# Expanding K and V for two heads at a time, and an output stage without its GpSimd copy, in an eight-core attention and LoRA-mixture layer

## What is computed

```
q    = rms(x @ wq_a.T) @ wq_b.T              # 32 heads of 64 + 64
ckv  = x @ wkv_a.T                           # 256 latent + 64 rotary key
kv   = rms(ckv[..., :256]) @ wkv_b.T         # 32 heads of 64 (k_nope) + 128 (v)
k    = concat(k_nope, rope(ckv[..., 256:]))  # the rotary part is shared by all heads
attn = softmax(causal(q @ k.T * scale)) @ v
x1   = ln(x + attn @ wo.T)
gate = softmax over the top 16 of 64 expert scores of x1
z    = (x1 @ A.T) * gate repeated over the 8 ranks of an expert
out  = ln(x1 + 2 * (z @ B.T))
```

## Time and profile before

| | us |
|---|---|
| median of 2 runs | 4685.25 (4610.16 and 4760.34) |
| the profiled execution | 4619.39 |
| its span, slowest core (core 6) | 4617.9 |
| spans of the other cores | 4577.5 to 4606.9 |
| stage D | about 1156 to 3394 |
| output stage | about 4494 to 4618 |

### The profile page before, as it was taken

One profiled execution on the slowest core, in us unless ns is written; L12 is line 12 of the kernel. 1 busy time (PEld: TensorE's weight loads), 2 busy tenths in 40 slices (PEclk: granted clock), 3 DMA queues, 4 the chain that ended last, 5 costly groups with the idle time before them and its releaser, 6 DMA issues.

```text
span 4617.9 us, 53437 instructions; the slowest of 8 cores (4577.5 to 4617.9 us)
## 1 busy us (share of the span) xinstructions
PE 2834.0 (61%) x19214; PEld 1381.3 (30%) x19214; DVE 1019.6 (22%) x1923; ACT 1232.6 (27%) x1280; POOL 402.4 (9%) x482
## 2 busy tenths in 40 slices
PE   2772744443666676666666666666678888718650
PEld 0220211111333343333333343333333333203110
DVE  0110000000232322222222323323310000161126
ACT  0000001111445444444444444444420000000110
POOL 4431002233000000000000000000010000000004
PEclk9886877777899989999999999999999999858765
DMA  8777240001100000000000000000053333110003
GB/s 123 110 99 108 38 71 2 0 0 27 19 1 1 1 1 1 1 1 1 1 1 1 1 1 1 1 1 1 1 82 83 86 82 85 41 38 0 0 5 141
DMA packets 76492, 145.66 MB, mean 32 GB/s; under 512 B 12306, under 2 KB 53396, under 8 KB 70228
## 3 DMA queue, kind: packets, MB, share of 16 engines
q0 software_dynamic: 65488, 107.90, 15.0%
q1 hardware_dynamic: 10756, 34.34, 1.9%
HBM read 233.31 MB, written 16.78 MB: 54 GB/s over the span
## 4 chain that ended last, share of the span: by engine, by line
PEldq 32%; issue 17%; PEld 15%; DVE 15%; ACT 7%; DMA 3%; another core or an unknown queue 3%; DVEq 2%; POOLq 2%; POOL 2%; ACTq 1%; SPq 0%
PEldq L267 32%; DVE AR L267 15%; ACT AR L267 7%; PEld mix L267 4%; PEld psE L267 3%; PEld sA L267 3%; DVEq L267 2%; POOLq L267 2%; POOL AR L267 2%; PEld psL L267 1%; ACTq L267 1%; DMA AR<-wqbT 1%; DMA AR<-xoT 1%; DMA out<-AR 1%
## 5 line engine op out<-in xcount | busy, mean ns | idle before, releaser
L267 PE MATMUL sA<-AR 128*128 128x128 bf16 (+2 forms) x3200 | 520.9, 285 | 194.1 <-DVEq L267 57.8
L267 PE MATMUL mix<-AR 128*128 128x129 bf16 x5120 | 411.8, 224 | 259.9 <-DVEq L267 172.5
L267 PE MATMUL psE<-AR 128*128 128x512 bf16 x2048 | 476.9, 396 | 15.1 <-issue 10.5
L267 PEld LDWEIGHTS mix<-AR 128*128 128x128 bf16 x5120 | 313.4, 99 | 573.6 <-DVEq L267 375.6
L267 PE MATMUL ptP<-idn,AR 128*128 128x128 bf16 x5120 | 404.7, 224 | 36.9 <-ACTq L267 36.5
L267 ACT ACTIVATE AR<-sB,consts 128x1024 bf16<-128x1024 f32 x320 | 357.2, 1116 | 147.5 <-PEq L267 118.9
L267 ACT ACTIVATE AR<-sA,consts 128x1024 bf16<-128x1024 f32 x320 | 357.2, 1116 | 93.9 <-PEq L267 73.6
L267 ACT COPY AR<-ptP 128x1024 bf16<-128x1024 bf16 x192 | 194.5, 1013 | 640.0 <-PEq L267 640.0
L267 ACT ACTIVATE AR<-AR 128x1024 bf16<-128x1024 bf16 (+3 forms) x76 | 76.5, 1007 | 1039.2 <-DVEq L267 1039.2
L267 PEld LDWEIGHTS ptP<-idn,AR 128*128 128x128 bf16 x5120 | 325.3, 100 | 47.8 <-ACTq L267 47.5
L267 PEld LDWEIGHTS sA<-AR 128*128 128x128 bf16 (+1 forms) x3200 | 196.5, 101 | 409.4 <-issue 385.1
(11 more groups left out here) (91 smaller groups left out, 1831.0 us busy)
## 6 DMA issues: line engine op xcount, KB each, us to landing
AR<-xT POOLq DMA_DIRECT2D x256, 128.0 KB, 10.5
AR<-wo_sta POOLq DMA_DIRECT2D x32, 1024.0 KB, 8.6
AR<-xoT SPq DMA_DIRECT2D x32, 512.0 KB, 8.2
out<-AR SPq DMA_DIRECT2D x32, 512.0 KB, 2.7
AR<-xoT POOLq DMA_DIRECT2D x32, 256.0 KB, 21.4
AR<-wqaT POOLq DMA_DIRECT2D x4, 2048.0 KB, 67.5
AR<-wqbT POOLq DMA_DIRECT2D x8, 1024.0 KB, 29.0
AR<-A_sta POOLq DMA_DIRECT2D x32, 128.0 KB, 10.2
```

The lines of the kernel that those rows point to most:

```text
L267: ins = getattr(h, meth)(*args, **kw)
```

## The change

1. `emit_expansion(h, bank_v, bank_k, gate)` expands heads h and h+1 together, and is called for even heads only. First comes all of V: 8 blocks with eight products of 256 columns each (both heads' value weights lie side by side), written to both banks of `bank_v`, then two ACT copies, one for each head. The next block waits for both copies. Then all of K: for each of the two heads 8 blocks with two products of 512 columns into one half of `bank_k`, and a DVE copy; each block waits for the copy of the block before, save the first of each head. K goes to the other score buffer, so that it first waits for the exponential of the iteration that was current (`gate`).
2. `Kf` and `Vx` get a third buffer (head modulo 3), so POOL copies `kpe` three times.
3. The weights are split on the host into `knT` (256 x 2048) and `vwT` (256 x 4096): four DMAs in place of two, of the same bytes.
4. In the output stage POOL's copy is gone: DVE subtracts straight from the bf16 tile. Even tiles are written by SP's queue as before, odd ones by POOL's.
5. Buffers that nothing used are gone.

```
-        def emit_expansion(h, bank):
-            hp = h % 2
-            war = tok_flash_done.get(h - 2)
...
-                if b >= 1:
-                    em.wait("pe", kn_ev[b - 1])
-                for c in range(2):
-                    em.opw("pe", [t_wkvb], "matmul", bank[0:64, 0:512],
...
-                em.op("dve", "tensor_copy", Kf[hp][0:64, b * 512:(b + 1) * 512],
-                      bank[0:64, 0:512])
+        def emit_expansion(h, bank_v, bank_k, gate):
+            war = [tok_flash_done.get(h - 3), tok_flash_done.get(h - 2)]
+            hp2 = [h % 3, (h + 1) % 3]
...
                 if b >= 1:
                     em.wait("pe", v_ev[b - 1])
                 for sub in range(4):
                     kk = b * 4 + sub
                     for c in range(2):
                         em.opw("pe", [t_wkvb], "matmul",
-                               bank[:, 512 + sub * 128: 512 + sub * 128 + 128],
+                               bank_v[:, sub * 256:(sub + 1) * 256],
                                cnorm[c][:, kk * 128:(kk + 1) * 128],
-                               wkvb_sb[c][:, h * 192 + 64: h * 192 + 192],
+                               Vw_sb[c][:, h * 128:(h + 2) * 128],
                                start=(c == 0), stop=(c == 1))
                 t_v = em.mark("pe")
...
+                for i in range(2):
+                    dst = Vx[hp2[i]][:, b * 4 * VSTRIDE:(b + 1) * 4 * VSTRIDE]
+                    dst = dst.rearrange("p (s w) -> p s w", w=VSTRIDE)[:, :, 0:128]
+                    em.op("act", "copy", dst, b3[:, :, i * 128:(i + 1) * 128])
                 v_ev[b] = em.mark("act")
                 ev.append(v_ev[b])
+            em.waits("pe", [gate])
+            for i in range(2):
+                prev = None
+                for b in range(8):
+                    if prev is not None:
+                        em.wait("pe", prev)
+                    for c in range(2):
+                        em.opw("pe", [t_wkvb], "matmul",
+                               bank_k[0:64, i * 512:(i + 1) * 512],
+                               Kn_sb[c][:, (h + i) * 64:(h + i) * 64 + 64],
+                               cnorm[c][:, b * 512:(b + 1) * 512],
+                               start=(c == 0), stop=(c == 1))
+                    t_kn = em.mark("pe")
+                    em.waits("dve", [t_kn, war[i], t_init, t_init_p])
+                    em.op("dve", "tensor_copy",
+                          Kf[hp2[i]][0:64, b * 512:(b + 1) * 512],
+                          bank_k[0:64, i * 512:(i + 1) * 512])
+                    prev = em.mark("dve")
+                    ev.append(prev)
...
-                if cur is not None and nxt["h"] != cur["h"]:
+                if cur is not None and nxt["h"] != cur["h"] and nxt["h"] % 2 == 0:
                     if r - 1 >= 0:
                         em.wait("pe", tok_exp[r - 1])
-                    emit_expansion(nxt["h"], scores[(r + 1) % 2])
+                    emit_expansion(nxt["h"], scores[(r + 1) % 2],
+                                   scores[r % 2], tok_exp[r])
...
-            em.op("pool", "tensor_copy", c32[p][:], Xw[:, ofc * 1024:(ofc + 1) * 1024])
-            cp_mark[ofc] = em.mark("pool")
-            em.wait("dve", cp_mark[ofc])
             if ofc >= 2:
                 em.waits("dve", [t_out[ofc - 2]])
-            em.op("dve", "tensor_tensor", c32[p][:], c32[p][:], meanB2, op=ALU.subtract)
+            em.op("dve", "tensor_tensor", c32[p][:],
+                  Xw[:, ofc * 1024:(ofc + 1) * 1024], meanB2, op=ALU.subtract)
...
-            em.wait("sp", o_mark[ofc])
-            t_out[ofc] = em.dma("sp", f"gout{p}",
+            q = "sp" if p == 0 else "pool"
+            em.wait(q, o_mark[ofc])
+            t_out[ofc] = em.dma(q, f"gout{p}",
                                 d["out"][ofc * 128:(ofc + 1) * 128, :], out_sb[p][:])
```

More of the change, by code:

```diff
@@ L103, in prepare_inputs @@
     wqbT = C(wq_b_p.reshape(H * QHD, 1024).T)
-    wkvbT = C(wkv_b.T)
+    wkvb3 = wkv_b.T.reshape(256, 32, 192)
+    knT = C(np.ascontiguousarray(wkvb3[:, :, 0:64]).reshape(256, 2048))
+    vwT = C(np.ascontiguousarray(wkvb3[:, :, 64:192]).reshape(256, 4096))
     wo_sta = C(np.transpose(wo.reshape(32, 128, 32, 128), (0, 3, 2, 1)))
@@ L132, in prepare_inputs @@
     shared = dict(
-        wkvaT=wkvaT, wqaT=wqaT, wqbT=wqbT, wkvbT=wkvbT, wo_sta=wo_sta,
+        wkvaT=wkvaT, wqaT=wqaT, wqbT=wqbT, knT=knT, vwT=vwT, wo_sta=wo_sta,
         A_sta=A_sta, B_sta=B_sta, WqT=WqT, keysT=keysT,
@@ L310, in build @@
     din("wqbT", (1024, 4096), F32)
-    din("wkvbT", (256, 6144), F32)
+    din("knT", (256, 2048), F32)
+    din("vwT", (256, 4096), F32)
     din("wo_sta", (32, 128, 32, 128), F32)
@@ L673, in _emit @@
             return
-    wkvb_sb = [ar.v(112 * KB + c * 12 * KB, 12 * KB) for c in range(2)]
-    Kf = [ar.v(136 * KB + i * 8 * KB, 8 * KB) for i in range(2)]
-    Vx = [ar.v(152 * KB + i * 8448, 8448) for i in range(2)]
+    Kn_sb = [ar.v(112 * KB + c * 4 * KB, 4 * KB) for c in range(2)]
+    Vw_sb = [ar.v(120 * KB + c * 8 * KB, 8 * KB) for c in range(2)]
+    Kf = [ar.v(136 * KB, 8 * KB), ar.v(144 * KB, 8 * KB),
+          ar.v(188 * KB, 8 * KB)]
+    Vx = [ar.v(152 * KB, 8448), ar.v(152 * KB + 8448, 8448),
+          ar.v(177 * KB, 8448)]
     P_sb = [ar.v(169 * KB + i * 2 * KB, 2 * KB) for i in range(2)]
     PT_sb = [ar.v(173 * KB + i * 2 * KB, 2 * KB) for i in range(2)]
[L680 to L686, removed]
     att_tm = ar.v(187 * KB, 256)
     rcp_c = ar.v(187 * KB + 256, 4, F32)
-    dbg_it_sb = ar.v(188 * KB, 16 * KB, F32)
     t_wo01 = None
@@ L706, in _emit @@
         for c in range(2):
-            t_wkvb = em.dma("pool", "gwkvb", wkvb_sb[c][:], d["wkvbT"][c * 128:(c + 1) * 128, :])
-        for i in range(2):
+            em.dma("pool", "gwkvb", Kn_sb[c][:], d["knT"][c * 128:(c + 1) * 128, :])
+            t_wkvb = em.dma("pool", "gwkvb", Vw_sb[c][:], d["vwT"][c * 128:(c + 1) * 128, :])
+        for i in range(3):
             em.op("dve", "memset",
@@ L738, in _emit @@
         fin_act_prev = [None]
-        def emit_expansion(h, bank):
-            hp = h % 2
-            war = tok_flash_done.get(h - 2)
+        def emit_expansion(h, bank_v, bank_k, gate):
+            war = [tok_flash_done.get(h - 3), tok_flash_done.get(h - 2)]
+            hp2 = [h % 3, (h + 1) % 3]
             ev = []
-            kn_ev = [None] * 8
+            em.waits("pe", [t_wkvb])
             v_ev = [None] * 8
-            em.waits("pe", [t_wkvb])
             for b in range(8):
-                if b >= 1:
-                    em.wait("pe", kn_ev[b - 1])
-                for c in range(2):
-                    em.opw("pe", [t_wkvb], "matmul", bank[0:64, 0:512],
[L752 to L756, removed]
-                em.op("dve", "tensor_copy", Kf[hp][0:64, b * 512:(b + 1) * 512],
-                      bank[0:64, 0:512])
-                kn_ev[b] = em.mark("dve")
-                ev.append(kn_ev[b])
                 if b >= 1:
@@ L773, in emit_expansion @@
[L773 to L776, removed]
+                em.waits("act", [t_v, war[0], war[1], t_init, t_init_p])
+                b3 = bank_v[:].rearrange("p (s w) -> p s w", w=256)
+                for i in range(2):
+                    dst = Vx[hp2[i]][:, b * 4 * VSTRIDE:(b + 1) * 4 * VSTRIDE]
+                    dst = dst.rearrange("p (s w) -> p s w", w=VSTRIDE)[:, :, 0:128]
+                    em.op("act", "copy", dst, b3[:, :, i * 128:(i + 1) * 128])
@@ L779, in emit_expansion @@
             tok_exp_ready[h] = ev
+            tok_exp_ready[h + 1] = ev
         def emit_qk(it):
@@ L783, in emit_qk @@
             par = it % 2
-            hp = cu["h"] % 2
+            hp = cu["h"] % 3
             if it - 2 >= 0:
@@ L794, in emit_qk @@
             tok_qk[it] = em.mark("pe")
-        emit_expansion(0, scores[0])
+        emit_expansion(0, scores[0], scores[1], None)
         emit_qk(0)
@@ L826, in _emit @@
                 em.waits("pe", [fin_act_prev[0]])
-                hpp = prev["h"] % 2
+                hpp = prev["h"] % 3
                 kbp = prev["kb"]
@@ L886, in _emit @@
             em.dma("sp", "gdbg", d["dbg_attn"], Q)
[L887 to L893, removed]
         if upto == "D":
@@ L1257, in _emit @@
         t_out = [None] * 32
-        cp_mark = [None] * 32
         o_mark = [None] * 32
@@ L1273, in _emit @@
             o_mark[ofc] = em.mark("dve")
-            em.wait("sp", o_mark[ofc])
-            t_out[ofc] = em.dma("sp", f"gout{p}",
+            q = "sp" if p == 0 else "pool"
+            em.wait(q, o_mark[ofc])
+            t_out[ofc] = em.dma(q, f"gout{p}",
                                 d["out"][ofc * 128:(ofc + 1) * 128, :], out_sb[p][:])
-        for p in range(2):
-            em.op("sp", "wait_ge", em.sem_dma[f"gout{p}"], 16 * em.ndma[f"gout{p}"])
+        for p, q in ((0, "sp"), (1, "sp")):
+            em.op(q, "wait_ge", em.sem_dma[f"gout{p}"], 16 * em.ndma[f"gout{p}"])
         if "gdbg" in em.sem_dma:
```

4 lines of the change are left out of this document (removed).

## The result

| | before | changed |
|---|---|---|
| median of all runs, us | 4724.86 (10 runs, from 4603) | 5127.62 (11 runs, from 5041) |
| ratio to before, 95% interval | | 1.0958 (1.0934 to 1.0982) |
| profiled execution, us | 4619.39 | 5048.51 |
| span of the slowest core, us | 4617.9 (core 6) | 5046.8 (core 1) |
| its mean granted clock | 0.871 | 0.797 |

The medians are over all executions, in some of which one die ran at a lower clock than the other; the ratio is of the undisturbed ones, and the profiled executions on both sides are such. The forecast for such an execution was 5063 us against 4619, a ratio of 1.096.

What follows compares the result with a forecast made beforehand. Stage D was taken as bound by the order of hand-offs between engines, with expansions whole in the chain. 4619.4 us, plus 448 for stage D (885 less 470, plus 33), less 4 for the output stage, gave 5063; range 4860 to 5170.

Steps and rivals of the forecast that it cites:

- The output stage, the landing of the odd tiles: Output stage: a store on POOL's queue lands in 4.3 us, two tiles take 7.3, the stage changes by -4 us.
- The estimate by the Trainium skill's figures for first bytes: Output stage: a POOL-queue store lands in 3.1 us, two tiles take 6.1, -22 us; not used in the sum.
- The V block's copies: V phase of a pair: two ACT copies of 0.59 in a row, 1.18 us, in blocks of 2.50 or 3.33.
- The half head behind: Stage D, behind a pair left at half clock: 2.2 us lost, between nothing and 4.1; 33 us over 15 pairs.
- all of stage D but two expansions ran at or near 1.00: Stage D before the change: reading of the clock, given as support for it holding after the change.
- An expansion stands whole in the chain: Stage D before the change: an expansion hides nothing, its 14.3 us stand whole; a head boundary without one costs nothing extra.
- The products and the K block: Pair expansion: eight 256-column products take 1.04 us or 1.87 at half clock; a K block 1.58 or 2.02.
- save PE nothing: V phase: 64 products of 256 columns for 128 of 128 save PE nothing, as the columns are the same.
- The clock: Pair expansion: the clock falls within the first V blocks, two taken at full, and stays down through K; pair 55.2 us.
- The third copy and the four DMAs: Before stage D: third kpe copy costs 0, hidden by the weight load; four DMAs cost 0 to +2 us, taken as 0.
- rival 1: Stage D: the clock holds, a pair costs 43.3 us, +223 us, total 4838 us; chance 0.10.
- rival 3: Stage D: not slower, copies fully beside products, some 18 us a pair, total 4408 us; decides under 29.4; chance 0.02.

Runs made afterwards that it cites:

- the filler kernel: The changed kernel with products whose results nobody reads added while PE waits in an expansion; copies and waits untouched: 4840.8 us median, ratio to before 1.0523.
- the interleaved order: The changed kernel with both heads' K products put back between V's, block by block, with its waits and buffers: 4511.6 us median, ratio to before 0.9786.

## Where the prediction failed, and what of it held

The mechanism held: lost overlap in each block, a clock that falls through it, and a price in the head behind. The steps that failed are terms of the sum that were mis-sized, the largest of them in the output stage:

- **The output stage, the landing of the odd tiles.** The step "I take 4.3 us" for a store on POOL's queue, chosen between loads of 3.7 and 5.0, failed: such a store lands in 2.9. Against that, 0.6 us pass from DVE's mark to POOL's issue, where the step had 0.1. Two tiles take 6.26 us instead of 7.3, and the stage is 18.5 us shorter instead of 4. The estimate by the Trainium skill's figures for first bytes ("DMA: Bandwidth & Descriptors", Specifications), 3.1 us to land and -22 in all, was nearer than the choice between the loads, though it too leaves out the 0.6.
- **The V block's copies.** 2.50 us at full clock and 3.33 at half were forecast; 2.39 to 2.45 and 3.22 were measured. The step that was off is the pair of ACT copies: 1.18 was taken as twice 0.59, while the row beside it already had two such instructions in 1.09; the two copies take 1.07. A pair was forecast at 55.2 us and most take 54.3; the first takes 56.4 against 56.9. All 16 take 869 us against 885, the 32 before took 466 against 470, and so the expansions add 403 us instead of 415.
- **The half head behind.** 2.2 us a pair was taken, between nothing and 4.1. It is 30.7 to 31.3 us in all 15 pairs, so that the upper end of the range is the rule, and head 7 was the typical case and not the extreme. The other end of the comparison was a good case: head 2 took 27.0 us, but the kernel before has 12 of its 32 half heads behind an expansion at a mean clock of 0.80 to 0.95 (27.5 to 31.1 us), and the mean of the 31 behind the first is 27.7. That "all of stage D but two expansions ran at or near 1.00" was too kind a reading, and it is the main reason why the rest of the stage grew by 41 us only and not by 15 times 4.1.

That the total came out within 15 us of the forecast is partly luck: -14.5 for the output stage and -12 for the expansions stand against +8 for the half heads, and the -12 and +15 of the stretches outside both nearly cancel.

What held:

- **An expansion stands whole in the chain.** The half head behind an odd boundary takes 27.1 to 27.5 us in 13 of 16 pairs of the changed kernel (28.1 to 28.3 in the others), with no pause where the odd head begins.
- **The products and the K block.** Eight products of 256 columns take 1.04 and 1.87 us, as interpolated. A K block was forecast at 2.02 us and takes 2.01; the phase 31.5 against 31.4; at full clock 1.58 against 1.58. Not so the aside that fewer V products "save PE nothing": two heads' sets of 128 columns take 2 x 0.61 us at full clock, the set of 256 columns 1.04. The sum itself had the 1.04.
- **The clock.** In 13 of 16 pairs it falls after two V blocks and stays at half through K, two pairs begin at half and stay there, and in one it comes back for 3.4 us. The experiments show that it is a consequence of the order, since filling the idle time alone brings it back. That it would be two V blocks had no row behind it; that was luck.
- **The third copy and the four DMAs.** Right at nothing: the three copies end at 1136.2 us, the first product waits for the weights until 1144.9, and that wait is as long as before.
- **The rivals.** The full clock of rival 1 is what the filler kernel has; it needed the fillers. That it took 4841 us where the rival had 4838 is no proof of each term: its V phase is 18.4 us against 18.8, its K phase 24.8 against 24.5, its half heads behind pairs are longer than 27 and its output stage is shorter. A pair under 29.4 us is what the interleaved order reaches, by taking out the waits on which rival 3 hung.

## What to carry to other kernels

Before two kinds of blocks that take turns are sorted by kind, ask what each one's copy out of PSUM runs beside. In a loop "products, copy, wait for the copy" with one buffer, the other kind's products are the cover, and fewer or larger instructions don't replace it. The clock comes on top: price the new loop at both of TensorE's levels, and price what follows it at the lower one for a while. And when a change has a gaining and a losing part, measure them apart: the gain in the output stage was real, and one queue made it larger.

## What the runs showed of the hardware

- Products whose results nobody reads can pay: 46 in each of 16 expansions, placed where PE would wait, took some 200 us off a 5041 us run by keeping the granted clock at or near 1.00.
- Work that follows a stretch at half clock pays for it, and not in one climb: behind each of 15 pairs the granted clock was 0.50 for 5 to 6 us, 1.00 for 3.4, 0.50 for 6.8 and then 1.00, and the half head took 31.0 us instead of 27.
- A 512 KB store lands in 2.9 us on GpSimd's queue and 2.7 on SyncE's, but GpSimd begins to issue it 0.6 us after DVE's mark, where SyncE needs 0.1.
- The clock can go either way in phases that look alike: with K blocks of 1.26 us the same K phase rose to full clock 6 us after its start in one pair and stayed at half to its end, 20 us, in the next.
- DVE's subtraction of 128 x 1024 takes 1.23 us with a bf16 or with an f32 first input, if the other input and the output are f32.
